# Decoder layers with a mixture of experts: the normalised rows are transposed last in a round of the token-expert stage, and the router products come one round later

## The chip, the cores and the metric

The kernel runs on one NeuronCore of one Trainium2 chip. The metric is the device time of one execution in microseconds (us). The engines that matter here are TensorE (PE: matmuls and transposes, with the weight loads apart as PEld), VectorE (DVE), ScalarE (ACT), GpSimd (POOL, which also issues the indirect transfers) and SyncE (SP, which issues the plain transfers). Each engine works through its own instructions in the order in which they are written, and waits at the head of its queue for the semaphores that the next instruction names.

## The reference

Three blocks on x of shape (4, 256, 256), each followed by a residual addition and a layer norm:

```
x = _layernorm(x + _L0_attn_ref(x, q_proj, k_proj, v_proj, o_proj))          # causal attention, 16 heads
x = _layernorm(x + _L0_xattn_ref(x, token_ids, ctx, ctx, ctx))               # expert by token id
x = _layernorm(x + _L0_ffn_ref(x, Wr, br, Wg, Wu, Wd))                       # top-1 expert by a router

# _L0_xattn_ref: expert_ids = min(clip(token_ids, 0, 12499) // 3125, 3); for the row's expert e
#   y = (silu(h @ Wg[e].T) * (h @ Wu[e].T)) @ Wd[e].T, here with all three = ctx (4, 256, 256)
# _L0_ffn_ref: probs = softmax(x @ Wr + br); top_w, top_idx = top_k(probs, 1)
#   out = top_w * ((silu(x @ Wg[top_idx]) * (x @ Wu[top_idx])) @ Wd[top_idx])
```

## The kernel before

The 1024 tokens are eight tiles of 128 rows. After attention (to about 118 us of the span) comes the **token-expert stage**, the second block of the reference. Six of the tiles have been scattered into rows that are sorted by expert and are read back as nine tiles of one expert each; the last two go through all four experts at once ("dense"). So the stage has NS = 11 tiles, of which numbers 3 and 6 are dense (DENSE_AT). Float32 products are made of three float16 products (hi*hi, hi*lo, lo*hi), so ScalarE writes a "hi" half and VectorE a "lo" half of every operand.

The stage is a software pipeline written out by hand. Each engine runs the same loop over rounds s = 0 to NS + 4; in round s the engines do different steps of different tiles, and every engine does its steps in the order of its own code:

- TensorE: T(s), two transposes of the tile's rows into bank 0 (L1513). T5(s-5), two transposes of the normalised rows into bank 5 (L1521), after a wait for `x2_rdy`. G(s-1), the gate product into bank 1 (L1263 through the helper `three`; six matmuls, for a dense tile twice six of 512 columns). T2(s-2), transposes of the gated rows into bank 2 (L1555; a dense tile: eight, L1499). D(s-3), the second product (L1263; a dense tile: 24 matmuls, L1576). R(s-5), the router product of four small matmuls (L1587), which waits for ScalarE's copy `x2T`.
- ScalarE: the hi half of T(s) (L670), the copy `x2T` of T5(s-5) (L677), SiLU of G(s-1) (L685; dense L693), the hi half of T2(s-2) (L701; dense L708). The latter waits until D of the sorted tile before has been done, since there is one buffer `hs_hi`.
- VectorE: the lo half of T(s) (L1105), SiLU times gate of tile s-1 (L1115; dense L1126), the lo half of T2(s-2) (L1134; dense L1090), the residual of tile s-3 (L1147), the normalisation of tile s-4 (L1152, which gives `x2_rdy`), the statistics of tile s-3 (L1156, L1158). Weight splits of the next stage (L552 on ScalarE, L779 on VectorE) lie in four places of the rounds.
- GpSimd: per tile the inverse deviation (L505, L506) that the normalisation waits for.

The router's work goes in two parts (PARTS): tiles 0 to 5 and tiles 6 to 10. For part 0, VectorE runs `logits` and `top_expert` (L825 to L843) at the start of round 11, ScalarE the exponentials (L661, with a table load) at the end of it, TensorE the counting product (L1256, L1257), and VectorE `top_weight` and `places` (L850 to L871) at the start of round 12; `places` gives `pos_rdy`. For part 1 all this follows after the last round. GpSimd's queue holds, in this order: the inverse deviations of tiles 0 to 8, the scatter of tile 0 (L512, waits for `places` of part 0), the inverse deviation of tile 9, the scatter of tile 1, the inverse deviation of tile 10, the scatters of tiles 2 to 5 and then those of tiles 6 to 10 (which wait for `places` of part 1). When all eleven have landed, the sorted tiles are read back and the third block runs (from about 195 us to the end), with TensorE busy nearly throughout.

Of the kernel before, what the change touches and what calls it, by code (L numbers as in the profile page):

```python
# [14 lines left out]
ALU, ACT, AX = mybir.AluOpType, mybir.ActivationFunctionType, mybir.AxisListType  # L15

P = 128
# [6 lines left out]
NK = D // P  # L24
# [24 lines left out]
NOWHERE = 8192.0  # L49
PARTS = ((0, 6), (6, NS))  # L50
# [14 lines left out]
def build(nc, x_tok, xT, ids, wqkvT, woT, ctxT, Wr, br, Wf, out):  # L65
    ctx = ExitStack()
    with ctx:
# [476 lines left out]
        def _(act):  # L544
# [118 lines left out]
            for s in range(NS + 5):  # L663
# [8 lines left out]
                i = s - 5  # L672
                if 0 <= i < NS:
                    act.wait_ge(x2T_rdy, i + 1)
                    if i >= 1:
                        act.wait_ge(lg_rdy, i)
                    a.activation(x2T, ps[:, 5, 0:D].rearrange("p (k t) -> p k t", k=NK),  # L677
                                 ACT.Copy).then_inc(x2T_sb, 1)
# [32 lines left out]
                if s - 3 in DENSE_AT:  # L711
                    split_hi(n)
                    n += 1
                for part, (_, last) in enumerate(PARTS[:-1]):
                    if s == last + 5:
                        exps_router(part)
# [51 lines left out]
        def _(dve):  # L768
# [325 lines left out]
            for s in range(NS + 5):  # L1094

                for part, (_, last) in enumerate(PARTS[:-1]):
                    if s == last + 5:
                        logits(part)
                        top_expert(part)
                    elif s == last + 6:  # L1100
                        top_weight(part)
                        places(part)
# [146 lines left out]
        def _(pe):  # L1249
# [253 lines left out]
            for s in range(NS + 5):  # L1503
# [11 lines left out]
                i = s - 5  # L1515
                if 0 <= i < NS:
                    pe.wait_ge(x2_rdy, i + 1)
                    if i >= 1:
                        pe.wait_ge(x2T_sb, i)
                    for k in range(NK):  # L1520
                        last = t.transpose(ps[:, 5, k * P:(k + 1) * P], XS[:, i, k * P:(k + 1) * P], identF[:, :])  # L1521
                    last.then_inc(x2T_rdy, 1)
# [56 lines left out]
                i = s - 5  # L1579
                if 0 <= i < NS:  # L1580
# [8 lines left out]
                    last.then_inc(lg_rdy, 1)  # L1589
                for part, (first, last) in enumerate(PARTS[:-1]):  # L1590
                    if s == last + 5:
                        pe.wait_ge(oh_rdy, part + 2)
                        count(PART_BANK[part], first, last)
# [121 lines left out]
```

## Time and profile before

| | us |
|---|---|
| three runs | 303.61, 306.0, 306.82 (median 306.0) |
| profiled execution, its own time | 303.86 |
| its span | 301.7 |
| around the span | 2.16 |
| PE / DVE / ACT / POOL busy | 239.1 / 193.3 / 135.8 / 66.8 |

"Busy" counts the time in which an engine has an instruction at work; matmuls overlap, so that a row's duration is longer than the step from its start to the next start, and that step is the price of an instruction in a full queue. In the timeline, the bracket at a row's end is the idle time of the engine just before it, and which instruction ended it. "PEclk" is the granted TensorE clock as a share of full speed: 1.00 is 2.4 GHz, and about 0.5 is 1.2 GHz.

### The profile page before, as it was taken

What the parts mean: (1) busy time and instruction counts of PE and PEld (TensorE: products, weight loads), DVE (VectorE), ACT (ScalarE), POOL (GpSimd) and SP (SyncE); (2) the same over time, 40 slices, a digit from 0 to 9 for tenths busy, and PEclk for the clock granted to TensorE, in tenths of its full rate; (3) what the DMA queues carried; (4) which work ended last, traced back from release to release, by engine and by line L of the source; (5) the groups of instructions that cost most, each with busy time, mean ns of one, the idle gap of its engine ahead of it and who ended that gap; (6) DMA issues with size and microseconds to landing.
All of it is one profiled execution on the core that took longest, in us unless ns stands there. A gap on an engine that the chain in (4) does not pass through costs nothing.

```text
span 301.7 us, 7078 instructions
## 1 busy us (share of the span) xinstructions
PE 239.1 (79%) x2714; PEld 192.2 (64%) x2730; DVE 193.3 (64%) x425; ACT 135.8 (45%) x229; POOL 66.8 (22%) x128
## 2 busy tenths in 40 slices
PE   4795598898988795778958575499696999999970
PEld 4363465665665563457747452199695999999960
DVE  4866858776797665576776835589645555555550
ACT  4460455765775964343534416177420333333300
POOL 8400000100032243122112286200022222222222
PEclk9797989999999999697999955999999999999996
DMA  6999216142043452411224902241000000000000
GB/s 207 332 281 299 74 45 253 59 139 70 3 141 107 118 165 98 130 27 45 77 66 134 412 24 88 79 121 41 2 20 0 21 13 21 21 20 20 2 8 14
DMA packets 17423, 28.62 MB, mean 95 GB/s; under 512 B 2733, under 2 KB 12974, under 8 KB 17392
## 3 DMA queue, kind: packets, MB, share of 16 engines
q1 hardware_dynamic: 16048, 25.28, 27.8%
q0 software_dynamic: 1344, 2.90, 2.7%
q8 instruction: 22, 0.36, 0.5%
q14 instruction: 9, 0.07, 0.1%
HBM read 19.43 MB, written 9.50 MB: 96 GB/s over the span
## 4 chain that ended last, share of the span: by engine, by line
PE 56%; DVE 21%; issue 8%; ACT 5%; DMA 4%; POOL 3%; SPq 1%; POOLq 0%; ACTq 0%; DVEq 0%
PE ps L1263 8%; PE ps L1632 7%; PE ps L1633 7%; PE ps L1634 7%; PE ps L1649 3%; PE ps L1651 3%; PE ps L1650 3%; PE ps L1334 3%; DVE arena L945 3%; PE ps L1373 2%; DVE wf_lo L779 2%; PE ps L1576 2%; PE ps L1521 2%; PE ps L1330 2%; DVE arena L1147 1%
## 5 line engine op out<-in xcount | busy, mean ns | idle before, releaser
L1632 PE MATMUL ps<-arena,wf_hi 128*128 128x128 f16 x352 | 60.2, 219 | 0.3 <-DVE arena L1175 0.3
L1633 PE MATMUL ps<-arena,wf_hi 128*128 128x128 f16 x352 | 60.3, 218 | 0.0
L1634 PE MATMUL ps<-arena,wf_lo 128*128 128x128 f16 x352 | 60.2, 217 | 0.0
L1633 PEld LDWEIGHTS ps<-arena,wf_hi 128*128 x352 | 34.3, 98 | 0.2
L1632 PEld LDWEIGHTS ps<-arena,wf_hi 128*128 x352 | 33.8, 96 | 0.9 <-issue 0.8
L1634 PEld LDWEIGHTS ps<-arena,wf_lo 128*128 x352 | 33.9, 96 | 0.0
L1649 PE MATMUL ps<-wf_hi,arena 128*128 x88 | 24.0, 273 | 5.9 <-DVE arena L1200 3.4
L779 DVE SCALAR_TENSOR_TENSOR wf_lo<-ring,wf_hi 128x1024 f16<-128x1024 f32 x17 | 20.6, 1220 | 12.5 <-ACT wf_hi L552 7.4
L735 ACT ACTIVATE arena<-ps 128x512 f32<-128x512 f32 x22 | 13.1, 595 | 29.7 <-PE ps L1634 29.7
L1650 PE MATMUL ps<-wf_lo,arena 128*128 x88 | 24.0, 273 | 0.0
L1651 PE MATMUL ps<-wf_hi,arena 128*128 x88 | 24.0, 273 | 0.0
L1263 PE MATMUL ps<-xT_hi,arena 128*128 (+1 forms) x88 | 23.1, 325 | 1.1 <-DVE arena L1115 1.1
L1184 DVE SCALAR_TENSOR_TENSOR arena<-ps,arena 128x512 f32<-128x512 f32 x22 | 15.2, 690 | 10.3 <-PE ps L1634 9.5
L742 ACT ACTIVATE arena<-arena 128x512 f16<-128x512 f32 x22 | 13.8, 629 | 16.6 <-DVE arena L1184 16.6
L1191 DVE TENSOR_TENSOR arena<-arena 128x512 f16<-128x512 f32 x22 | 15.2, 690 | 8.8 <-ACT arena L742 8.8
L945 DVE TENSOR_REDUCE arena<-ps 128x4 f16<-128x1024 f32 x16 | 19.6, 1223 | 1.6 <-PE ps L1334 1.6
L1263 PE MATMUL ps<-arena,xT_hi 128*128 128x512 f16 (+1 forms) x64 | 16.5, 348 | 2.7 <-DVE arena L900 1.9
L529 POOL TENSOR_SCALAR veps<-mv 128x1 f32<-128x1 f32 x11 | 2.5, 225 | 71.1 <-DVE mv L1206 71.1
L552 ACT ACTIVATE wf_hi<-ring 128x1024 f16<-128x1024 f32 x17 | 17.7, 1052 | 0.1
L599 ACT ACTIVATE arena<-ps 128x1024 f32<-128x1024 f32 x16 | 16.5, 1033 | 1.1 <-PE ps L1357 0.7
L940 DVE TENSOR_REDUCE arena<-ps 128x4 f16<-128x512 f32 x16 | 11.0, 689 | 8.0 <-PE ps L1334 7.8
L1334 PE MATMUL ps<-arena 128*128 128x128 f16 x144 | 13.8, 236 | 1.7 <-DVE wf_hi L926 1.0
(223 smaller groups left out, 568.1 us busy)
## 6 DMA issues: line engine op xcount, KB each, us to landing
ring<-Wf SPq DMA_DIRECT2D x17, 512.0 KB, 3.7
sorted<-fill SPq DMA_DIRECT2D x1, 4515.0 KB, 21.9
arena<-Wf SPq DMA_DIRECT2D x7, 512.0 KB, 7.2
arena<-sorted SPq DMA_DIRECT2D x20, 129.0 KB, 2.5
sorted<-fill SPq DMA_DIRECT2D x1, 1161.0 KB, 6.6
ring<-xT SPq DMA_DIRECT2D x4, 256.0 KB, 4.8
X<-x_tok SPq DMA_DIRECT2D x1, 1024.0 KB, 7.7
ring<-ctxT SPq DMA_DIRECT2D x2, 512.0 KB, 3.8
```

The source lines that it names most:

```text
L552: a.activation(chunk_dst(ORDER[n], True), src, ACT.Copy, scale=W_SCALE).then_inc(c_hi, 1)
L599: a.activation(Pf[n % 2][:, 1:3], ps[:, 4:6, :], ACT.Exp, scale=DK ** -0.5).then_inc(exped, 1)
L779: v.scalar_tensor_tensor(out=chunk_dst(ORDER[n], False), in0=staged(n)[0], scalar=W_SCALE, in1=chunk_dst(ORDER[n], True), op0=ALU.mult, op ...
L945: v.tensor_reduce(dst[:, 1], ps[:, 1:3, :].rearrange("p c (a k) -> p a c k", a=G), AX.XY, ALU.max, negate=True).then_inc(maxed, 1)
L1263: last = t.matmul(dst, xs(k), ws(k), start=(k == 0 and m == 0), stop=(k == nk - 1 and m == 2))
L1334: last = t.matmul(ps[:, bank, i * P:(i + 1) * P], q[:, h, qt * P:(qt + 1) * P], k[:, h // 2, kt * P:(kt + 1) * P], start=not diag, stop=(n ...
L1632: t.matmul(dst, hi, a_hi[p][:, k], start=k == 0, stop=False)
L1633: t.matmul(dst, hi, a_lo[p][:, k], start=False, stop=False)
L1634: last = t.matmul(dst, lo, a_hi[p][:, k], start=False, stop=k == NK - 1)
L1649: t.matmul(ps[:, 7, 0:D], hs[:, c], hi, start=c == 0, stop=False)
L1650: t.matmul(ps[:, 7, 0:D], hs[:, c], lo, start=False, stop=False)
L1651: last = t.matmul(ps[:, 7, 0:D], ls[:, c], hi, start=False, stop=c == NF - 1)
```

## The change

The constant LOGIT_LAG = 6 takes the place of the 5 in the length of the rounds and in the places of the router's work. Three things move. On TensorE the transposes T5(s-5) go from behind T(s) to the end of round s, and the router product in round s is that of tile s-6. On ScalarE the copy `x2T` of tile s-5 goes from the second place of the round to the last. On VectorE, ScalarE and TensorE the router work of part 0 (`logits`, `top_expert`, exponentials, count, `top_weight`, `places`) comes one round later, and there is one round more. GpSimd's and SyncE's instructions and their order stay as they are.

```
@@ -47,6 +47,7 @@
 NEG = -3.0e38
 PAD_TOKEN = 4096.0
 NOWHERE = 8192.0
+LOGIT_LAG = 6
 PARTS = ((0, 6), (6, NS))
 PART_BANK = (6, 7)
 AHEAD3 = 3
@@ -660,7 +661,7 @@
                 act.wait_ge(lg_sb, part + 1)
                 a.activation(ex[:, first:last, :], lg[:, first:last, :], ACT.Exp).then_inc(ex_rdy, 1)
 
-            for s in range(NS + 5):
+            for s in range(NS + LOGIT_LAG):
                 if s < NS:
                     act.wait_ge(a2T, s + 1)
                     if s >= 2:
@@ -669,13 +670,6 @@
                             act.wait_ge(bz, 2 * dense_before(s - 1))
                     a.activation(a_hi[s % 2], ps[:, 0, 0:D].rearrange("p (k t) -> p k t", k=NK),
                                  ACT.Copy).then_inc(a2hi, 1)
-                i = s - 5
-                if 0 <= i < NS:
-                    act.wait_ge(x2T_rdy, i + 1)
-                    if i >= 1:
-                        act.wait_ge(lg_rdy, i)
-                    a.activation(x2T, ps[:, 5, 0:D].rearrange("p (k t) -> p k t", k=NK),
-                                 ACT.Copy).then_inc(x2T_sb, 1)
                 i = s - 1
                 k, j = (sorted_of(i), dense_of(i)) if 0 <= i < NS else (None, None)
                 if k is not None:
@@ -711,8 +705,15 @@
                 if s - 3 in DENSE_AT:
                     split_hi(n)
                     n += 1
+                i = s - 5
+                if 0 <= i < NS:
+                    act.wait_ge(x2T_rdy, i + 1)
+                    if i >= 1:
+                        act.wait_ge(lg_rdy, i)
+                    a.activation(x2T, ps[:, 5, 0:D].rearrange("p (k t) -> p k t", k=NK),
+                                 ACT.Copy).then_inc(x2T_sb, 1)
                 for part, (_, last) in enumerate(PARTS[:-1]):
-                    if s == last + 5:
+                    if s == last + LOGIT_LAG:
                         exps_router(part)
             exps_router(len(PARTS) - 1)
             a.activation(sg[:, 0:1], identF[:, 0:1], ACT.Silu)
@@ -1091,13 +1092,13 @@
                                 h_hi[:, 4 * half:4 * half + 4], ALU.subtract).then_inc(bhlo, 1)
 
             inv = 1 / W_SCALE
-            for s in range(NS + 5):
+            for s in range(NS + LOGIT_LAG):
 
                 for part, (_, last) in enumerate(PARTS[:-1]):
-                    if s == last + 5:
+                    if s == last + LOGIT_LAG:
                         logits(part)
                         top_expert(part)
-                    elif s == last + 6:
+                    elif s == last + LOGIT_LAG + 1:
                         top_weight(part)
                         places(part)
                 if s < NS:
@@ -1500,7 +1501,7 @@
                                        identF[:, :])
                 last.then_inc(bhT, 1)
 
-            for s in range(NS + 5):
+            for s in range(NS + LOGIT_LAG):
                 if s < NS:
                     k = sorted_of(s)
                     if k is not None:
@@ -1512,14 +1513,6 @@
                     for k in range(NK):
                         last = t.transpose(ps[:, 0, k * P:(k + 1) * P], XS[:, s, k * P:(k + 1) * P], identF[:, :])
                     last.then_inc(a2T, 1)
-                i = s - 5
-                if 0 <= i < NS:
-                    pe.wait_ge(x2_rdy, i + 1)
-                    if i >= 1:
-                        pe.wait_ge(x2T_sb, i)
-                    for k in range(NK):
-                        last = t.transpose(ps[:, 5, k * P:(k + 1) * P], XS[:, i, k * P:(k + 1) * P], identF[:, :])
-                    last.then_inc(x2T_rdy, 1)
                 i = s - 1
                 k, j = (sorted_of(i), dense_of(i)) if 0 <= i < NS else (None, None)
                 if k is not None or j is not None:
@@ -1576,7 +1569,7 @@
                             last = t.matmul(ps[:, (3, 4)[i % 2], 0:D], xs[:, c], ws[:, c * D:(c + 1) * D],
                                             start=(c == 0 and m == 0), stop=(c == NF - 1 and m == 2))
                     last.then_inc(y2, 1)
-                i = s - 5
+                i = s - LOGIT_LAG
                 if 0 <= i < NS:
                     if i == 0:
                         pe.wait_ge(in_r, 32)
@@ -1587,8 +1580,16 @@
                         last = t.matmul(ps[:, bank, col * E:(col + 1) * E], x2T[:, k], wr_sb[:, k, :],
                                         start=(k == 0), stop=(k == NK - 1))
                     last.then_inc(lg_rdy, 1)
+                i = s - 5
+                if 0 <= i < NS:
+                    pe.wait_ge(x2_rdy, i + 1)
+                    if i >= 1:
+                        pe.wait_ge(x2T_sb, i)
+                    for k in range(NK):
+                        last = t.transpose(ps[:, 5, k * P:(k + 1) * P], XS[:, i, k * P:(k + 1) * P], identF[:, :])
+                    last.then_inc(x2T_rdy, 1)
                 for part, (first, last) in enumerate(PARTS[:-1]):
-                    if s == last + 5:
+                    if s == last + LOGIT_LAG:
                         pe.wait_ge(oh_rdy, part + 2)
                         count(PART_BANK[part], first, last)
             pe.wait_ge(oh_rdy, len(PARTS) + 1)
```

The places in the queues, as rows of the compiled kernels. First TensorE where round 9 ends and round 10 begins, before the change: the last matmul of a dense second product (L1576), the router product R(4), the transposes T(10) (L1513), then T5(5) (L1521), and the gate product G(9) (L1263; ISA and REGISTER_ALU set its address).

```order
L1576 MATMUL ps<-xT_hi,arena 128x256
L1587 MATMUL ps<-wr_sb,arena 128x4 x2
L1513 MATMUL ps<-identF,arena 128x128 x2
L1521 MATMUL ps<-identF,arena 128x128 x2
L1263 ISA
L1263 MATMUL ps<-xT_hi,arena 128x256
```

The same place after the change, where the lines are L1569 for the second product, L1580 for the router product (now R(3)), L1589 for T5 (now T5(4)), L1514 for T(10) and L1264 for G(9):

```order
L1569 MATMUL ps<-xT_hi,arena 128x256
L1580 MATMUL ps<-wr_sb,arena 128x4 x2
L1589 MATMUL ps<-identF,arena 128x128 x2
L1514 MATMUL ps<-identF,arena 128x128 x2
L1264 ISA
L1264 MATMUL ps<-xT_hi,arena 128x256
```

T5 now stands behind the products of its round, and nothing stands between T(10) and G(9). 

Second, ScalarE's queue in rounds 7 to 9 before the change: a_hi (L670), the copy x2T (L677), SiLU (L685), then the hi half of T2 (L708 for the dense tile, L701 else).

```order
L670 ACTIVATE arena<-ps 128x256
L677 ACTIVATE arena<-ps 128x256
L685 ACTIVATE arena<-ps 128x256
L708 ACTIVATE arena<-ps 128x512 x2
L670 ACTIVATE arena<-ps 128x256
L677 ACTIVATE arena<-ps 128x256
L685 ACTIVATE arena<-ps 128x256
L701 ACTIVATE arena<-ps 128x256
```

After the change (a_hi is L671, SiLU L679, the dense hi half L702, the other L695, the copy x2T L713):

```order
L671 ACTIVATE arena<-ps 128x256
L679 ACTIVATE arena<-ps 128x256
L702 ACTIVATE arena<-ps 128x512 x2
L713 ACTIVATE arena<-ps 128x256
L671 ACTIVATE arena<-ps 128x256
L679 ACTIVATE arena<-ps 128x256
L695 ACTIVATE arena<-ps 128x256
```

The copy has moved behind both steps that it stood ahead of.

Third, the end of the stage on TensorE before the change, from T5(8) on: the second product D(10), then R(8), T5(9), R(9), T5(10), R(10) and the count of part 1.

```order
L1521 MATMUL ps<-identF,arena 128x128 x2
L1263 MATMUL ps<-xT_hi,arena 128x256
L1263 MATMUL ps<-xT_lo,arena 128x256
L1263 MATMUL ps<-xT_hi,arena 128x256 x2
L1263 MATMUL ps<-xT_lo,arena 128x256
L1263 MATMUL ps<-xT_hi,arena 128x256
L1587 MATMUL ps<-wr_sb,arena 128x4 x2
L1521 MATMUL ps<-identF,arena 128x128 x2
L1587 MATMUL ps<-wr_sb,arena 128x4 x2
L1521 MATMUL ps<-identF,arena 128x128 x2
L1587 MATMUL ps<-wr_sb,arena 128x4 x2
```

After the change, from the count of part 0 on (L1257, L1258): D(10), R(7), T5(8), R(8), T5(9), R(9), and T5(10) and R(10) behind them.

```order
L1257 MATMUL ps<-oh,before 128x24
L1258 MATMUL ps<-oh,ones 128x24
L1264 MATMUL ps<-xT_hi,arena 128x256
L1264 MATMUL ps<-xT_lo,arena 128x256
L1264 MATMUL ps<-xT_hi,arena 128x256 x2
L1264 MATMUL ps<-xT_lo,arena 128x256
L1264 MATMUL ps<-xT_hi,arena 128x256
L1580 MATMUL ps<-wr_sb,arena 128x4 x2
L1589 MATMUL ps<-identF,arena 128x128 x2
L1580 MATMUL ps<-wr_sb,arena 128x4 x2
L1589 MATMUL ps<-identF,arena 128x128 x2
L1580 MATMUL ps<-wr_sb,arena 128x4 x2
```

The count of part 0 now stands ahead of D(10), one round later than before, and the order of the last three tiles' transposes and router products among themselves is the same.

## Rows read from the trace of the kernel before

**Rows 1.** Waits between 118 and 185 us: waiter <- releaser: total us, times, longest.

```profile
PE ps L1521 <- DVE arena L1152: 11.5, 10, 2.1
```

**Rows 2.** Busy time and granted clock by stretch (stretch, length, busy by engine, PEclk, DMA).

```profile
136.20:139.70 3.50, 3.44 (x17) 3.04 (x18) 1.26 (x5) 1.35 (x3) 0.79 (x2) 0.51 0.12 48
139.70:173.60 33.90, 24.71 (x206) 20.50 (x203) 25.95 (x78) 15.62 (x34) 5.70 (x15) 1.00 0.43 154
173.60:184.20 10.60, 6.00 (x26) 4.56 (x26) 5.31 (x28) 4.04 (x8) 7.73 (x10) 0.51 0.15 51
```

**Rows 3.** Timeline, TensorE, rounds 5 and 6: start, us, line, idle before.

```profile
133.79 0.38 PE L1513 MATMUL ps<-identF,arena 128*128 128x128 f32 x2
136.26 0.69 PE L1521 MATMUL ps<-identF,arena 128*128 128x128 f32 x2 [2.09 <-DVE arena L1152]
...
140.72 0.42 PE L1513 MATMUL ps<-identF,arena 128*128 128x128 f32 x2
```

**Rows 4.** Timeline, VectorE, around the dense tile 3.

```profile
133.57 1.65 DVE L1126 SCALAR_TENSOR_TENSOR arena<-ps,pick,arena 128x256 f32<-128x256 f32 x4
135.14 0.41 DVE L1134 TENSOR_TENSOR arena<-ps,arena 128x256 f16<-128x256 f32 x1
```

**Rows 5.** Timeline, TensorE, rounds 7 to 10, at full clock.

```profile
146.97 0.38 PE L1263 MATMUL ps<-xT_hi,arena 128*128 128x512 f16 x1
...
149.56 0.38 PE L1555 MATMUL ps<-identF,arena 128*128 128x128 f32 x2
...
153.44 1.04 PE L1499 MATMUL ps<-identF,arena 128*128 128x128 f32 x8
154.32 0.27 PE L1263 MATMUL ps<-xT_hi,arena 128*128 x1
...
157.86 0.44 PE L1521 MATMUL ps<-identF,arena 128*128 128x128 f32 x2 [2.10 <-DVE arena L1152]
158.13 0.27 PE L1263 MATMUL ps<-xT_hi,arena 128*128 x1
...
158.79 0.38 PE L1555 MATMUL ps<-identF,arena 128*128 128x128 f32 x2
159.00 0.27 PE L1576 MATMUL ps<-xT_hi,arena 128*128 128x256 f16 x1
...
161.62 0.51 PE L1587 MATMUL ps<-wr_sb,arena 128*128 128x4 f32 x4
161.99 0.42 PE L1513 MATMUL ps<-identF,arena 128*128 128x128 f32 x2
```

**Rows 6.** Timeline, all engines, rounds 11 and 12: from D(8) to the next T5.

```profile
167.47 0.27 PE L1263 MATMUL ps<-xT_hi,arena 128*128 x1
...
168.79 1.28 ACT L661 ACT_TABLE_LOAD   x1
168.81 0.42 DVE L1134 TENSOR_TENSOR arena<-ps,arena 128x256 f16<-128x256 f32 x1 [0.23 <-ACT arena L701]
...
169.94 0.44 PE L1521 MATMUL ps<-identF,arena 128*128 128x128 f32 x2 [1.25 <-DVE arena L1152]
170.09 0.22 ACT L661 ACTIVATE ex<-lg 128x24 f32<-128x24 f32 x1
...
170.35 0.16 DVE L850 TENSOR_SCALAR off<-valid 128x6 f32<-128x6 f32 x1
```

**Rows 7.** Timeline, all engines, the tail: places of part 0 to the scatter of tile 6.

```profile
172.42 0.17 DVE L871 TENSOR_TENSOR pos_i<-pos,off 128x6 int32<-128x6 f32 x1
...
173.44 1.10 POOL L512 DMA_INDIRECT sorted<-arena,pos_i  x1 [2.04 <-DVE pos_i L871]
...
174.90 0.57 POOL L506 TENSOR_TENSOR rstd<-veps,minus_half 128x1 f32<-128x1 f32 x1
...
177.85 0.41 DVE L1152 TENSOR_SCALAR arena<-arena,mv,rstd 128x256 f32<-128x256 f32 x1 [1.01 <-POOL rstd L506]
...
185.02 0.97 POOL L512 DMA_INDIRECT sorted<-arena,pos_i  x1 [1.97 <-DVE pos_i L871]
```

More of the change, by code:

```diff
@@ L49 @@
 NOWHERE = 8192.0
+LOGIT_LAG = 6
 PARTS = ((0, 6), (6, NS))
@@ L661, in exps_router @@
                 a.activation(ex[:, first:last, :], lg[:, first:last, :], ACT.Exp).then_inc(ex_rdy, 1)
-            for s in range(NS + 5):
+            for s in range(NS + LOGIT_LAG):
                 if s < NS:
@@ L671, in _ @@
                                  ACT.Copy).then_inc(a2hi, 1)
[L672 to L678, printed above, removed]
                 i = s - 1
@@ L713, in _ @@
                     n += 1
+                i = s - 5
+                if 0 <= i < NS:
+                    act.wait_ge(x2T_rdy, i + 1)
+                    if i >= 1:
+                        act.wait_ge(lg_rdy, i)
+                    a.activation(x2T, ps[:, 5, 0:D].rearrange("p (k t) -> p k t", k=NK),
+                                 ACT.Copy).then_inc(x2T_sb, 1)
                 for part, (_, last) in enumerate(PARTS[:-1]):
-                    if s == last + 5:
+                    if s == last + LOGIT_LAG:
                         exps_router(part)
@@ L1093, in _ @@
             inv = 1 / W_SCALE
-            for s in range(NS + 5):
+            for s in range(NS + LOGIT_LAG):
                 for part, (_, last) in enumerate(PARTS[:-1]):
-                    if s == last + 5:
+                    if s == last + LOGIT_LAG:
                         logits(part)
                         top_expert(part)
-                    elif s == last + 6:
+                    elif s == last + LOGIT_LAG + 1:
                         top_weight(part)
@@ L1501, in dense_T @@
                 last.then_inc(bhT, 1)
-            for s in range(NS + 5):
+            for s in range(NS + LOGIT_LAG):
                 if s < NS:
@@ L1514, in _ @@
                     last.then_inc(a2T, 1)
[L1515 to L1522, printed above, removed]
                 i = s - 1
@@ L1578, in _ @@
                     last.then_inc(y2, 1)
-                i = s - 5
+                i = s - LOGIT_LAG
                 if 0 <= i < NS:
@@ L1589, in _ @@
                     last.then_inc(lg_rdy, 1)
+                i = s - 5
+                if 0 <= i < NS:
+                    pe.wait_ge(x2_rdy, i + 1)
+                    if i >= 1:
+                        pe.wait_ge(x2T_sb, i)
+                    for k in range(NK):
+                        last = t.transpose(ps[:, 5, k * P:(k + 1) * P], XS[:, i, k * P:(k + 1) * P], identF[:, :])
+                    last.then_inc(x2T_rdy, 1)
                 for part, (first, last) in enumerate(PARTS[:-1]):
-                    if s == last + 5:
+                    if s == last + LOGIT_LAG:
                         pe.wait_ge(oh_rdy, part + 2)
```

## The prediction

> **What bounds the kernel now.** I read the waits of the token-expert stage first, then its timeline on TensorE, then the rows of the tail across all engines. TensorE stands still for T5, the transposes of the normalised rows, in ten of eleven rounds, 11.5 us in all, and every time VectorE's normalisation (L1152) ends the wait [rows 1]. The longest waits are 2.09 and 2.10 us [rows 3, 5]. The reader is to see in rows 6 what such a wait consists of: TensorE begins D(8) at 167.47, ScalarE and VectorE turn the gated rows into halves (VectorE from 168.81), then VectorE does residual and normalisation, and T5(7) begins at 169.94. T5 stands near the head of a round, so it waits for the last link of the round before, and the products behind it, which need none of that, wait too. From 172.42 on another chain sets the end: `places` of part 0, then GpSimd's queue (scatter, inverse deviation of tile 9, scatter, inverse deviation of tile 10), then the normalisation of tile 10 at 177.85, its router product, and the scatter of tile 6 at 185.02 [rows 7]. Everything behind that scatter keeps its instructions and its order, so I take it to shift as one piece.
>
> **Prices.** From starts of neighbours in a full queue at full clock [rows 5]: a gate product G and a second product D of a sorted tile (the same six matmuls) 0.66 us (158.13 to 158.79); a dense gate product 2.59 (146.97 to 149.56); a dense second product 2.62 (159.00 to 161.62); T2 0.21; dense T2 0.88 (153.44 to 154.32); a router product R 0.37 (161.62 to 161.99); T5 0.27 (157.86 to 158.13), and T, which has the same shape, as much. A semaphore from one engine to the next I count as 0.05 us (168.81 to 169.94 holds three links in line and leaves no more).
>
> **Round 5 after the change.** T(5) begins at 133.79 as before [rows 3] and costs 0.27. G(4) then needs only the first half of VectorE's dense gating, four instructions from 133.57 in 1.65 us, so half of it by 134.40 [rows 4]: it runs from 134.45 to 135.11. The dense T2 needs the lo half of tile 2, ready at 135.14 + 0.41 = 135.55 [rows 4]: from 135.60, 0.88 long. D(2) adds 0.66, T5(0) 0.27, so T(6) begins at 137.41 instead of 140.72 [rows 3]: 3.3 us earlier. The wait of 2.09 has shrunk to two of 0.39 and 0.49, R(0) has gone to the next round (0.37), and the stretch at half clock from 136.2 to 139.7 (0.51, [rows 2]) is assumed gone. That is worth 3.50 x 0.49 = 1.7 us of the 3.3. Two ends: it stays (0 of the 1.7), or it goes (all). I take the latter, because the stretch followed directly on the idle 2.09 us and TensorE now idles 0.9 us there in two pieces; the rest of the stage ran at 1.00 although TensorE waited in it [rows 2].
>
> By the Trainium skill ("TensorE: Matmul & The Clock Gate", Part 1: The HAM clock gate) the half rate is the default and activity of the engine releases it, so by the page too the early stretch would go; but it speaks against the thin end of the stage, where the engine has little to do from round 11 on and could fall to half rate sooner. The trace agrees with the first half in that the 0.51 follows a wait [rows 2, 3]; it does not bear out that every such wait lowers the clock, since the 2.10 us at 157.86 did not [rows 2, 5].
>
> **Rounds 6 to 11.** With no wait for T5, a round costs TensorE what it issues. Round 6: T, G, T2, dense D, R, T5 = 0.27 + 0.66 + 0.21 + 2.62 + 0.37 + 0.27 = 4.40. Round 7 (dense gate): 4.37. Round 8 (dense T2): 3.11. Round 9 (dense D): 4.40. Round 10: 2.44. Round 11, without T: 2.17. Sum 20.89, so round 12 begins at 158.30; before, it began with T5(7) at 169.94 [rows 6].
>
> Is that cover real? The next thing to be late is T2 or D, which wait for the lo half of the tile before. From D's start to that half takes 168.81 + 0.42 + 0.05 - 167.47 = 1.81 us [rows 6]. Between D and the next T2, TensorE now issues D, R, T5, T and G = 2.23 us in rounds 6 to 10, and 1.96 without T in round 11: cover of 0.42 and 0.15 us. In round 12 neither T nor G is left: 1.30 us, so T2(10) waits 0.5. T5 itself has the whole round as cover for residual and normalisation. If the cover were gone, each round would pay the difference. The copy `x2T` costs nothing in its new place: what is queued behind it on ScalarE is a_hi of the next round and the SiLU of the next G, and both need TensorE work that stands behind T5 anyway. R(s-6) finds the copy done a round ago.
>
> **Part 0 of the router, one round later.** Round 12: 158.30 + 0.5, T2(10) 0.21, D(9) 0.66, R(6) 0.37, T5(7) begins at 160.04 and ends at 160.48. ScalarE must copy it (0.4) before the exponentials, table load and all 1.30 + 0.22 [rows 6]: done at 162.4. VectorE: D(8) begins at 157.00, so its lo half at 157.00 + 1.34 = 158.34, and 1.54 us later (168.81 to 170.35, [rows 6]) its next round: 159.88. `logits` and `top_expert` are eight small instructions; the twelve from 170.35 to 172.42 [rows 6, 7] have a step of 0.19, so 1.5 us: 161.4. Residual, normalisation and statistics, 1.54 again: 162.95. The exponentials are ready, so `top_weight` and `places` run, L871 starting 2.07 later at 165.0. Before: 172.42. So 7.4 us earlier; without the added round it would have been some 3 us more (the logits and 1.54 of VectorE).
>
> **The tail.** GpSimd's scatter of tile 0 waits for `places`, and the inverse deviation of tile 9 is queued behind it, then the next scatter, then that of tile 10. Before, the normalisation of tile 10 began 177.85 - 172.42 = 5.43 us after L871, with GpSimd as releaser [rows 7]. Now tile 9's has to wait for the same chain: it begins 3.1 us after L871 (174.90 + 0.57 + 0.05 - 172.42), at 168.1. Tile 10's statistics follow it by 169, while GpSimd is still in the second scatter. So tile 10 is normalised at 165.0 + 5.43 = 170.4, and R(9), at half clock about 1 us, ends by 170.7, before T5(10) can start at 170.9. The new wait of some 4 us ahead of T5(9) is parallel to this chain and costs nothing. From there to the scatter of tile 6 it is 7.17 us as before [rows 7]: 177.6 against 185.02.
>
> **Sum.** -7.4 us against the profiled execution, 303.86, gives 296.5. That execution is a low one: it and the three runs (303.61, 306.0, 306.82) have a mean of 305.1, 1.2 above it. I do not know which level the next runs take and add the 1.2: 297.7. Against the median of 306.0 the same sum would give 298.6.
>
> **Rivals.**
> 1. The forecast, chance 0.69: 7.4 us less, own range 295.5 to 299.
> 2. Part of it is eaten, chance 0.19. Either half clock stays in round 5 or comes at the thin end: +1.7 for the stretch of rows 2, and up to +2.2 where round 11 runs at half rate. Or the cover of 0.42 us is too small: 0.3 us in each of six rounds is +1.8. Times 299.4 to 302. For: the clock did fall twice in this stage [rows 2]; VectorE is busy 25.95 of 33.9 us [rows 2], and my rounds leave it less air. Against: VectorE's share of the 31.7 us from T(6) to L871 is 24.3 us, and I give that work 27.6.
> 3. The waits only move, chance 0.07: T2 and D wait for their halves about 1 us in each round, and the added round eats the rest; 302.9 to 306.
> 4. The change is slower, chance 0.05. The mechanism is GpSimd's queue: if the rounds kept their length, `places` of part 0 would come one round later, 3.6 us (T5, G, T2 = 1.14 and 169.94 - 167.47 = 2.47, [rows 6]), and with it scatter, tile 9, tile 10 and part 1. That gives 307.5 by the profiled execution, 308.7 at the level of my forecast. It decides as soon as rounds 5 to 12 give back less than 3.6 of the 11.5 us. Against it: G needs nothing of the normalisation, by code and by rows 4.
>
> That the change does nothing is part of 3; the order of TensorE's rows excludes that T5 still holds up its own round.
>
> **Range and chances.** 295.0 takes the lower level of the runs with 1.5 us more than the sum; 301.5 takes the half clock and most of the lost cover. What a measurement here can tell from no change is about 1%, 3 us. Faster by over 1% (below 302.9): 0.88. Within: 0.07. Slower: 0.05.
>
> **What would show it.** TensorE's wait for L1152 is gone in rounds 5 to 12 and there is one long wait, about 4 us, ahead of T5(9). T(6) begins near 137.4, L871 of part 0 near 165.0, and the scatter of tile 6 near 177.6; the granted clock is 1.00 from 136.2 on. Wrong would be: waits of T2, D or G for VectorE of more than 0.3 us in each round, 0.5 in PEclk after 134, L871 later than 168, or more than 5.5 us from it to the normalisation of tile 10.

## The result, and the profile after

The changed kernel takes 294.31 us (median of 294.12 to 296.42, four runs) against 306.41 us of the kernel before (303.61 to 309.97) in the same measurement. The ratio is 0.9717, 95% interval 0.9676 to 0.9759: 2.8% faster. (The ratios here compare undisturbed runs only, so they are not the quotients of the medians.) On a second chip it took 299.05 us (298.75 to 299.61) against 304.2, ratio 0.9845 (0.977 to 0.9919). The sign is the same, the size is not, and the experiments below have to say why.

| | before, profiled | after, profiled |
|---|---|---|
| its own time / span | 303.86 / 301.7 | 294.23 / 292.2 |
| T(0) begins | 120.85 | 120.20 |
| T(0) to T(5) | 12.94 | 11.67 |
| T(5) to the scatter of tile 6 | 51.23 | 43.56 |
| from there to the last scatter | 5.11 | 5.11 |
| last scatter to the end | 111.57 | 111.66 |

T(5), with which round 5 begins, is the last thing on TensorE ahead of the first moved instruction. So 7.67 of the 9.5 us between the spans lie where the change is, and 1.9 us ahead of it, in code that both kernels share.

The waits of TensorE for the normalisation answer to [rows 1]; the first row shown is GpSimd's wait for the places. Waits from 118 to 178 us of the changed kernel (waiter <- releaser: total us, times, longest):

```profile
POOL sorted L513 <- DVE pos_i L872: 7.0, 2, 5.1
...
PE ps L1589 <- DVE arena L1153: 4.2, 2, 4.0
```

11.5 us in ten waits have become 4.2 us in two, and the long one of 4.0 stands in the tail, beside GpSimd's chain, where it costs nothing of its own. Here is TensorE's timeline in round 5 and at the start of round 6, which answers to [rows 3]:

```profile
131.87 0.38 PE L1514 MATMUL ps<-identF,arena 128*128 128x128 f32 x2
...
132.68 0.28 PE L1264 MATMUL ps<-xT_hi,arena 128*128 x1 [0.43 <-DVE arena L1127]
...
133.60 1.09 PE L1500 MATMUL ps<-identF,arena 128*128 128x128 f32 x8
...
135.18 0.38 PE L1589 MATMUL ps<-identF,arena 128*128 128x128 f32 x2
135.40 0.38 PE L1514 MATMUL ps<-identF,arena 128*128 128x128 f32 x2
```

T(5) to T(6) is 3.53 us; it was 6.93. The one wait that these rows name is for VectorE's dense gating (L1127), ahead of G(4). A second, of some 0.26 us ahead of the dense T2, can be read from the starts only (133.60 against 132.68 + 0.66, the price of G). Here are all waits of TensorE between 133 and 166 us that the same timeline shows, one after the other:

```profile
156.73 0.44 PE L1548 MATMUL ps<-identF,arena 128*128 128x128 f32 x2 [0.38 <-DVE arena L1135]
159.44 0.19 PE L1257 MATMUL ps<-oh,before 128*128 128x24 f16 x1 [1.00 <-DVE oh L844]
159.86 0.27 PE L1264 MATMUL ps<-xT_hi,arena 128*128 x1 [0.21 <-DVE arena L1135]
161.77 0.61 PE L1580 MATMUL ps<-wr_sb,arena 128*128 128x4 f32 x4 [0.47 <-ACT arena L713]
```

From 134 to 156 there is none: rounds 6 to 11 run nearly on what TensorE issues. The tail, all engines, answers to [rows 7]:

```profile
162.88 0.17 DVE L872 TENSOR_TENSOR pos_i<-pos,off 128x6 int32<-128x6 f32 x1
...
163.89 1.09 POOL L513 DMA_INDIRECT sorted<-arena,pos_i  x1 [5.05 <-DVE pos_i L872]
...
165.34 0.57 POOL L507 TENSOR_TENSOR rstd<-veps,minus_half 128x1 f32<-128x1 f32 x1
165.95 0.41 DVE L1153 TENSOR_SCALAR arena<-arena,mv,rstd 128x256 f32<-128x256 f32 x1 [2.57 <-POOL rstd L507]
...
166.42 0.69 PE L1589 MATMUL ps<-identF,arena 128*128 128x128 f32 x2 [4.04 <-DVE arena L1153]
...
168.30 0.41 DVE L1153 TENSOR_SCALAR arena<-arena,mv,rstd 128x256 f32<-128x256 f32 x1 [1.38 <-POOL rstd L507]
...
175.43 0.97 POOL L513 DMA_INDIRECT sorted<-arena,pos_i  x1 [1.92 <-DVE pos_i L872]
```

The scatter of tile 0 has been waited for (5.05 us), the inverse deviation of tile 9 runs behind it, and VectorE (2.57) and TensorE (4.04) wait in turn. The clock by stretch answers to [rows 2]; the third number from the end is PEclk:

```profile
134.00:140.00 6.00, 6.00 (x58) 5.51 (x57) 5.93 (x16) 3.39 (x8) 1.58 (x4) 1.00 0.10 41
140.00:158.00 18.00, 17.62 (x150) 14.77 (x148) 16.32 (x46) 10.31 (x25) 3.98 (x11) 1.00 0.49 162
...
164.00:176.00 12.00, 4.95 (x18) 3.06 (x19) 5.68 (x32) 5.06 (x8) 8.46 (x11) 0.50 0.13 43
```

The stretch at half clock (1.2 GHz) in round 5 is gone, and TensorE is busy 17.62 of 18 us in the middle of the stage.

### The profile page after: what moved, and what is told of

It is laid out like the page before. It is cut to its first block, busy times and chain, and to the rows that moved or that the text cites. A ratio compares the mean times of both kernels' runs of the same rounds, so it can differ in the third digit from the quotient of the medians.

```text
span 292.2 us, 7078 instructions
## 1 busy us (share of the span) xinstructions
PE 233.1 (80%) x2714; PEld 188.0 (64%) x2730; DVE 192.3 (66%) x425; ACT 135.0 (46%) x229; POOL 66.8 (23%) x128
## 4 chain that ended last, share of the span: by engine, by line
PE 56%; DVE 18%; issue 9%; DMA 5%; ACT 5%; POOL 4%; SPq 1%; POOLq 0%; DVEq 0%; ACTq 0%
PE ps L1264 8%; PE ps L1633 7%; PE ps L1634 7%; PE ps L1635 7%; PE ps L1650 3%; PE ps L1652 3%; PE ps L1651 3%; PE ps L1335 3%; PE ps L1374 2%; DVE arena L946 2%; PE ps L1569 2%; POOL sorted L513 2%; PE ps L1331 2%; DVE arena L941 2%; ACT wf_hi L553 1%
## 5 line engine op out<-in xcount | busy, mean ns | idle before, releaser
L1264 PE MATMUL ps<-xT_hi,arena 128*128 (+1 forms) x88 | 20.5, 299 | 1.1 <-DVE arena L1127 0.4
L1264 PE MATMUL ps<-arena,xT_hi 128*128 128x512 f16 (+1 forms) x64 | 15.8, 337 | 2.5 <-DVE arena L901 1.8
L534 POOL DMA_INDIRECT out<-arena,out_i x11 | 12.0, 1091 | 13.8 <-DVE arena L1213 13.8
```

Source lines behind the costliest of these rows:

```text
L1264: last = t.matmul(dst, xs(k), ws(k), start=(k == 0 and m == 0), stop=(k == nk - 1 and m == 2))
```

## The experiments

**All profiled executions in one table.** The four columns, with the 5.1 us from the scatter of tile 6 to the last scatter (5.09 to 5.13 in all rows), make up the whole span. "Stage" is from T(5) to the scatter of tile 6; "rest" is from the last scatter to the end, and its code is the same in all rows except where dummies were put in.

```
                             T(0) at  T(0)-T(5)  stage   rest    half clock in the rest at
before                        120.9     12.94    51.23   111.57  -
before, dummies in stage 3    121.3     13.03    51.34   111.56  -
before, dummies in rounds     121.0     11.70    49.51   111.55  -
before, GpSimd reordered      119.8     10.99    52.83   113.83  192, 216
after                         120.2     11.67    43.56   111.66  -
after, again                  122.0     11.71    43.62   115.36  186 to 192, 210
after, dummies in stage 3     121.2     12.95    43.66   113.16  222
T5 early                      120.3     10.99    56.19   111.60  -
copy early                    121.3     10.99    58.11   113.12  220 to 224
no lag                        120.7     11.00    46.64   113.56  186, 210
T5 twice                      118.9     12.93    45.09   113.63  184 to 188, 208
lo half twice                 121.4     12.94    46.47   113.63  188, 212
GpSimd: scatters last         120.3     10.99    41.43   113.04  180 to 186
GpSimd, dummies               120.4     12.94    40.96   111.62  -
```

The stage repeats to 0.1 us where the code is the same (two rows of the kernel before, three of the changed one). The two columns beside it do not: 11.0 to 13.0, and 111.6 to 115.4. So the stage is what the theories are judged by, and the times of whole runs say less. That the two rows of the kernel before agree is in part luck: the first row has half clock from 136.2 to 139.7 us, behind the wait in round 5, the second from 156 to 160 us, behind the one in round 9, one stretch each. "Dummies" are matmuls that only keep TensorE busy; nothing reads their results.

### The changed kernel again

No edit.

> The changed kernel itself, on the same chip as the next three, so that they can be held against it. All theories: the ratio to the kernel before is 0.972 again. In the trace the stretch from T(5) to the scatter of tile 6 is 43.6 us (51.2 before). What happens ahead of T(5) is the same code in both kernels: if the first profile's 1.9 us there was only the phase in which the clock rose, this stretch differs from run to run; if it belongs to the change, T(5) begins at 131.9 again and not near 133.8.

Measured: 299.05 us against 304.2 (ratio 0.9845, where 0.972 was expected). The stage took 43.62 us, as in the first profile (43.56). T(5) began at 133.7, as in the kernel before (133.8) and not at 131.9: the 1.9 us ahead of the stage were not the change's. The kernel was slower than on the first chip in the rest: 115.36 us instead of 111.66. The profile of this run there (busy by engine; the third number from the end is PEclk):

```profile
186.00:192.00 6.00, 5.22 (x34) 3.69 (x33) 3.84 (x4) 2.27 (x3) 0.00 (x0) 0.51 0.43 114
192.00:208.00 16.00, 16.00 (x271) 15.83 (x269) 12.49 (x18) 12.01 (x20) 0.00 (x0) 0.97 0.19 52
208.00:210.40 2.40, 0.04 (x1) 0.00 (x0) 2.40 (x4) 1.29 (x2) 0.00 (x0) 0.92 0.00 0
210.40:213.00 2.60, 2.52 (x12) 1.80 (x13) 0.51 (x1) 0.00 (x0) 0.00 (x0) 0.50 0.00 0
```

After each of two waits TensorE worked for some us at half clock. The same waits stand in the first profile, 3.2 us for the scatters and 2.4 us ahead of the first down product, and there the clock stayed at full speed behind them.

### T5 back at the head of the round, the rest as changed

```
                     last.then_inc(a2T, 1)
+                i = s - 5
+                if 0 <= i < NS:
+                    pe.wait_ge(x2_rdy, i + 1)
...
-                i = s - 5
-                if 0 <= i < NS:
-                    pe.wait_ge(x2_rdy, i + 1)
```

(with the two transposes of T5 behind the wait in both places)

> The changed kernel with T5 back behind T(s) on TensorE; the router products stay one round later and ScalarE's copy stays last. Theory (T5's wait at the head of the round was the brake): the gain is gone, the wait for the normalisation is back in every round, and the added round costs a little: 0 to +1 us against the kernel before, near 306. Rival (the gain comes from ScalarE's order, or from the router products that no longer wait for their copy): most of the 8 to 9 us stays, near 298.

Measured: 309.69 us (305.95 to 324.67), ratio 1.0198 (1.0085 to 1.0312): slower than before. Waits from 128 to 180 us:

```profile
PE ps L1522 <- DVE arena L1153: 15.0, 9, 4.8
```

The wait is back, 15.0 us of it. Without the move on TensorE nothing of the gain is left; the rival falls. I had expected at most 1 us of loss. In the trace T(5) to L872 is 42.8 us against 38.6 of the kernel before: the router's part 0 comes one round later, the price that the forecast's fourth rival put at 3.6 us, and here nothing pays for it. But the clock fell to 0.5 around 136 and 156, two stretches against the one of the kernel before. The kernel before with GpSimd's queue reordered (below) has two such stretches at the same places and takes 39.4 us over this distance. Against that row the added round costs 3.4 us, and the rest of the 4.2 goes with the second stretch.

### ScalarE's copy back in second place

```
                                  ACT.Copy).then_inc(a2hi, 1)
+                i = s - 5
+                if 0 <= i < NS:
+                    act.wait_ge(x2T_rdy, i + 1)
...
-                i = s - 5
-                if 0 <= i < NS:
-                    act.wait_ge(x2T_rdy, i + 1)
```

(with the copy x2T behind the wait in both places)

> The changed kernel with ScalarE's copy x2T back in second place of the round, ahead of SiLU and of the hi half; TensorE as changed. Theory (each engine waits at the head of its queue): the copy of round s waits for T5 at the end of TensorE's round, with SiLU(s-1) and the hi half behind it, so that all engines run in turn: from T(5) to the scatter of tile 6 some 59 us instead of 43.6, the kernel 7 to 9 us slower than before, near 314. Rival (ScalarE is only 45% busy and its order hardly matters): within 2 us of the changed kernel, near 298.

Measured: 311.41 us, ratio 1.0281 (1.0193 to 1.037); the stage took 58.11 us, 14.5 more than with the copy last. Waits from 128 to 180 us:

```profile
ACT arena L678 <- PE ps L1589: 29.2, 9, 6.3
DVE arena L1116 <- ACT arena L686: 13.0, 7, 3.9
...
PE ps L1264 <- DVE arena L1116: 6.1, 5, 1.4
```

The forecast of this run was a stage of some 59 us. ScalarE (133.6 us busy of 308.6) stands 29.2 us in front of the copy, VectorE waits for the SiLU behind it, and TensorE's next gate product waits for VectorE. The move on TensorE needs the move on ScalarE: the low busy share of ScalarE did not make its order harmless. The clock stood at half between 149 and 156 us too; how much of the 14.5 us that is was not measured.

### Router products in the same round, directly behind T5

```
-LOGIT_LAG = 6
+LOGIT_LAG = 5
```

(and on TensorE the block of T5 stands ahead of that of R, both at the end of the round)

> The changed kernel without the later router products: T5 behind D, then at once R of the same tile, LOGIT_LAG = 5. Theory: R waits for ScalarE's copy in every round, about 0.5 us with TensorE idle, and one round is saved: of the gain of 7.7 us some 3 us is left, near 303. Rival (the lag only costs a round, since part 0 comes later): faster than the changed kernel by up to 3 us, near 294.

Measured: 299.55 us, ratio 0.9872 (0.9797 to 0.9948). The stage took 46.64 us: 3.1 more than changed, 4.6 less than before. Waits of the trace from 128 to 180 us:

```profile
PE ps L1588 <- ACT arena L713: 6.7, 11, 1.3
```

Eleven waits for the copy, 6.7 us, against one round saved; neither kernel has half clock between T(5) and 164 us. The rival, that the lag is pure cost, falls: the lag is worth 3.1 us net. The expectation had put 4.7 us on it (3 left of 7.7), so its sign was right and its size half too large.

### GpSimd: the scatters behind the inverse deviations

```
-            for i in range(NS - 2):
+            for i in range(NS):
                 inv_std2(i)
-            scatter3(0, 0)
-            inv_std2(NS - 2)
-            scatter3(0, 1)
-            inv_std2(NS - 1)
```

(and the loop behind it then issues all scatters.)

> The changed kernel with GpSimd's queue reordered: all inverse deviations first, then the scatters of tiles 0 to 10. Theory (in the tail, the scatters of tiles 0 and 1 stand ahead of the inverse deviations of tiles 9 and 10, and that chain now sets the end): normalisation of tile 10 some 2.8 us earlier, the scatters then follow one another without a gap, and the last one begins 2.5 us earlier: 2 to 3 us faster than the changed kernel, ratio to the kernel before near 0.964. Rival (the chain is hidden behind the last products, or the scatters are the bound anyway): no difference to the changed kernel, 0.972.

Measured: 292.43 us, ratio 0.9641 (0.9584 to 0.9698), and a stage of 41.43 us, 2.1 less than in the changed kernel (2.5 expected). GpSimd's timeline, where the first of these scatters is that of tile 0:

```profile
164.09 0.57 POOL L507 TENSOR_TENSOR rstd<-veps,minus_half 128x1 f32<-128x1 f32 x1
164.92 1.15 POOL L513 DMA_INDIRECT sorted<-arena,pos_i  x1 [0.27 <-issue]
166.38 0.97 POOL L513 DMA_INDIRECT sorted<-arena,pos_i  x1 [0.30 <-issue]
...
177.86 0.97 POOL L513 DMA_INDIRECT sorted<-arena,pos_i  x1 [0.30 <-issue]
```

From L868 (162.32, the places of part 0) to the normalisation of tile 10 (164.69) it now takes 2.4 us instead of 5.4. The gap ahead of the scatter of tile 6 has gone, and the eleven scatters run one behind the other at 1.28 us: now GpSimd's issue is what ends last. The rival of a hidden chain falls.

### The same on the kernel before

> The same reordering of GpSimd's queue in the kernel before. Theory: there the normalisations of tiles 9 and 10 came late for another reason too (the products), so that little is to be had: -0.5 to +0.5 us, ratio 1.00. Rival (the scatters ahead of the inverse deviations cost the kernel before as much as the changed one): 2 to 3 us faster, ratio 0.992.

Measured: 305.58 us (301.74 to 307.1) against 303.75 (301.5 to 308.35); no ratio is on record, and the spreads overlap. The stage took 52.83 us instead of 51.23, 1.6 more, where -0.5 to +0.5 was expected. Here the order is no gain. The first of the eleven scatters now starts at 175.8, behind the inverse deviation of tile 10, and that of tile 6 comes at 183.6, 1.63 us after its places (L867 at 181.95) where it was 0.96 in the kernel before: 0.7 us is the queue's. The other 0.9 had come by those places, and what differs up to there is a half-clock stretch around 156, which the first profile does not have. The same edit is worth 2.1 us in one kernel and nothing in the other. The traces show why: in the old one GpSimd could begin the inverse deviation of tile 9 at 171.98 only, on the release of its statistics, 1.8 us after the places of part 0 (L867 at 170.19); in the changed kernel those statistics are written at 160.74, 2.1 us ahead of the places, and the scatter of tile 0 is all that the inverse deviation still stands behind.

### T5 issued twice

```
-                    for k in range(NK):
+                    for k in (0, 1, 0, 1):
```

> The changed kernel with the two transposes of T5 issued twice in each round (the same data into the same place, output unchanged): 0.27 us more of TensorE's issue time a round. Theory (TensorE's issue time now sets the round, by the prices of the forecast): eight rounds ahead of L872 pay it, +1.9 to +2.5 us against the changed kernel. Rival (VectorE sets the round now): below 0.7 us.

Measured: 297.83 us (294.28 to 300.4); the ratio to the kernel before, 0.972, is that of the changed kernel, so that the price shows in the trace alone: the stage took 45.09 us, 1.5 more than changed. The step from T5 to T in the trace is 0.47 us instead of 0.25, so that each doubling costs 0.22, not 0.27, and T(5) to T(10) grows from 19.73 to 20.60 us in five rounds, by 0.2 in four of them. Of the 1.5 us, 1.0 have come by L872; the other 0.5 are T5(9) and T5(10) at half clock. Both my figure (1.9 to 2.5) and the rival's (below 0.7) miss. The direction speaks for TensorE as the bound of rounds 5 to 8, where the extra time comes through whole (round 9 takes 4.53 us before and 4.55 with it); in rounds 11 and 12 most of it disappears in the wait for the lo half (0.16 us left of 0.38 in the trace).

### The lo half written twice

```
+                    link(v.tensor_tensor(hs_lo, ps[:, 2, 0:D].rearrange("p (k t) -> p k t", k=NK),
+                                         hs_hi, ALU.subtract))
                     v.tensor_tensor(hs_lo, ps[:, 2, 0:D].rearrange("p (k t) -> p k t", k=NK),
                                     hs_hi, ALU.subtract).then_inc(h2lo, 1)
```

> The changed kernel with VectorE's lo half of each sorted tile written twice, the first time waited for: 0.43 to 0.46 us more of VectorE a round, just ahead of the lo half that T2 and D wait for (output unchanged). Theory (this link has a cover of 0.42 us in rounds with T and G behind D, 0.15 in round 11 and none after): +2.5 to +3.3 us, most of it in rounds 10 to 13 and in the round with the dense T2. Rival (VectorE has slack, 16.3 us busy of 18): below 1 us. Rival (VectorE is the bound): 9 x 0.45 = 4 us.

Measured: 301.36 us (ratio 0.9894, 0.9837 to 0.995); the stage took 46.47 us, 2.9 more, as the theory said. The timeline of TensorE has these waits for the written halves (L1137), and none for them between the second and the third:

```profile
137.04 1.09 PE L1502 MATMUL ps<-identF,arena 128*128 128x128 f32 x8 [0.55 <-DVE arena L1137]
148.85 1.09 PE L1502 MATMUL ps<-identF,arena 128*128 128x128 f32 x8 [0.31 <-DVE arena L1137]
...
161.61 0.44 PE L1550 MATMUL ps<-identF,arena 128*128 128x128 f32 x2 [0.83 <-DVE arena L1137]
...
165.20 0.37 PE L1266 MATMUL ps<-xT_hi,arena 128*128 x1 [0.65 <-DVE arena L1137]
```

From T to T, rounds 6, 7 and 9 take 4.35, 4.30 and 4.53 us with and without the doubling: the cover takes it whole there. The 2.9 us come from round 5 (1.0, VectorE being late with the dense gating too), the round with the dense T2, and rounds 11 to 13, where no T or no G lies between D and the next T2. I had not named round 5. Both rivals fall (below 1 us, and 4 us).

### The kernel before with dummies in two waits of its rounds

```
                 i = s - 5
+                if i in (0, 4):
+                    keep_warm(8, wf_hi[:, 0:512], bank=5)
```

> The kernel before with 8 dummy matmuls ahead of T5(0) and of T5(4), in the two waits of about 2.1 us; order unchanged. It prices the clock alone. Theory: the stretches at half clock in rounds 5 and 9 are gone; from T(5) to the scatter of tile 6 it takes 49.3 to 49.9 us instead of 51.2 (52.8 in the run with both stretches), so the clock is 1.3 to 1.9 us of the 7.7. Rival (most of the gain is the clock that stays high when TensorE no longer waits): 45 us or less.

Measured: 303.17 us, ratio 0.9983 (0.9932 to 1.0033); the stage took 49.51 us, 1.7 less than before. No half clock in rounds 5 to 11:

```profile
127.00:170.00 43.00, 35.69 (x275) 27.43 (x274) 32.86 (x96) 21.07 (x46) 8.03 (x18) 1.00 0.36 125
```

So the clock is 1.7 us of the 7.67, as the forecast had it, and 6.0 are left for the order. The rival, that the clock is most of it, falls. In the time of whole runs the 1.7 us disappear in the spread.

### Dummies in the third stage, after and before

```
-            keep_warm(2 * WARM_GAP, wf_hi[:, 0:512])
+            keep_warm(26, wf_hi[:, 0:512])
...
                 if i == 0:
+                    keep_warm(8, wf_hi[:, 0:512], bank=5)
                     pe.wait_ge(c_lo, NCH)
```

> The changed kernel with idle TensorE time of the third stage filled: 26 instead of 16 dummy matmuls behind pos_rdy of part 1, and 8 ahead of the first down product (whose wait for VectorE's split was 2.4 us). Nothing else moves. Theory (from the scatter of tile 10 to the end the same code took 111.7, 113.0 and 115.4 us, because half clock followed these two waits in some executions and not in others): the stretches at half clock around 188 and 210 us are gone, the remainder is 111.7 us, and the runs lie near 294 with a small spread. Rival (the difference between 294 and 299 of the changed kernel is another chip or another cause): 297 to 300 as on the second chip, with or without dummies.

> The kernel before with the same dummy matmuls in the third stage. Theory: it too runs at its lower level, 302 to 304, and the two filled kernels differ by what the change does in its own stage, 7.6 us or 2.5%, with less spread than the unfilled pair. Rival (part of the gain of the first measurement lay in the third stage): the two filled kernels differ by 5 us or less.

Measured: 296.99 us for the changed kernel (295.24 to 298.31), where near 294 was expected and 297 to 300 was the rival's; 303.86 for the one before (300.67 to 305.53, ratio 1.0007). In both profiles the clock stays up at the two filled places, but in the changed kernel half clock came at another one, behind the wait of the third down product for VectorE. TensorE's timeline there:

```profile
222.42 0.39 PE L1651 MATMUL ps<-wf_hi,arena 128*128 x1 [2.74 <-DVE arena L1201]
```

That wait stands in every profile, and in no other one is there half clock behind it. So the expectation that the spread would go fails: the dummies move the place, and whether fewer such stretches come cannot be told from one profile each. The two filled kernels differ by 6.9 us in their medians, and by 7.7 in the stage (51.34 against 43.66), so that the second expectation's rival (5 us or less) falls.

### Both additions together

The dummies of the third stage, 5 more ahead of T5(9), and only the scatter of tile 0 ahead of the inverse deviation of tile 10:

```
-            for i in range(NS - 2):
+            for i in range(NS - 1):
                 inv_std2(i)
             scatter3(0, 0)
-            inv_std2(NS - 2)
-            scatter3(0, 1)
             inv_std2(NS - 1)
```

> The changed kernel with three additions: GpSimd's queue with only the scatter of tile 0 ahead of the inverse deviation of tile 10 and all other scatters behind it, the dummies of the third stage, and 5 dummies in the wait ahead of T5(9). Theory: L872 to the normalisation of tile 10 in 3.2 us instead of 5.4; the last scatter begins 3.5 us earlier than in the changed kernel, 45 us after T(5) instead of 48.7; the remainder is 111.7 us, so 290 us. Rival (the scatters are now the bound, 11 x 1.28 us from L872 on, whatever is ahead of them): no better than the run with all scatters last, 46.5 us.

Measured: 294.2 us (292.13 to 296.72), ratio 0.9708 (0.9573 to 0.9843), where 290 was expected. The places of part 0 (L870) to the normalisation of tile 10 took 3.1 us, as expected (3.2), and the rest 111.62. But the stage took 40.96 us, only 0.5 less than with all scatters last: T(5) to the last scatter is 46.1 us instead of 46.5, not the 45 that I had put on it. The scatters now follow one another without a gap and are the bound, as the rival said. This is the shortest stage of all kernels, but its time is not better than the 292.43 us of the simpler edit, measured on another chip with an overlapping spread; which of the two is faster is open.

## Why the prediction was right, step by step

**What bounded the kernel: right.** T5's wait for the last link of the round before was the brake. Putting T5 back brings the wait (15.0 us) and takes the whole gain away.

**Round 5: right.** Forecast 3.62 us from T(5) to T(6), measured 3.53. The half clock was taken to go, worth 1.7; it went, and the dummies in the kernel before measure 1.7. Both waits of the forecast came, split otherwise (0.54 and 0.26 us for 0.39 and 0.49, read from starts and prices): G(4) began 1.12 us after the dense gating (forecast 0.88), the dense T2 2.04 us after it (forecast 2.03), each counted from the start of L1127 at 131.56.

**Rounds 6 to 11: right to 0.1 us.** The forecast gave 20.89 us from T(6) to the start of round 12. T5(6) began at 155.94 and takes a step of 0.25, so TensorE was free at 156.19, 20.79 us after T(6) at 135.40. The cover of 0.42 us held too, as the doubled lo half shows. In round 12, T2(10) began at 156.73, 0.54 us after TensorE was free, forecast 0.5 (the bracket of 0.38 counts from the end of T5's own duration).

**One round later: right.** L872 came 31.01 us after T(5), forecast 31.2 (165.0 - 133.79).

**Tail: right.** L872 to the normalisation of tile 10 took 5.42 us, forecast 5.43; the new wait of 4.04 us ahead of T5(9) cost nothing, forecast "some 4". From there to the scatter of tile 6, 7.13 against 7.17.

**The sum: 7.4 forecast, 7.67 measured** for what the change touches. Against the 306.0 us shown, the ratio 0.9717 gives 297.3 us, 0.4 from the forecast of 297.7. That closeness is in part luck: the ratio stands for 8.7 us, of which the changed stage holds 7.67, and the rest lies in code that both kernels share.

**What was mis-sized is the level, not the change.** The first measurement's own median, 294.31, is 3.4 us below 297.7 and 0.7 below the low end. The step that failed is the last: I added 1.2 us because the profiled execution seemed a low one, and took everything ahead of T(5) and behind the scatter as fixed. Neither is. In the table of the profiled executions, T(0) to T(5) varies by 2.0 us and the rest by 3.8 us in shared code, and wherever it is longer, the trace has half clock there. The mean granted clock of each timed run tells it too: the kernel before takes 301.0 to 302.5 us at a mean clock of 0.945 to 0.952 and 303.2 to 305.4 at 0.934 to 0.936; the changed kernel takes 294.1 to 294.4 at 0.945 to 0.950, 296.4 at 0.934 and 298.8 to 299.6 at 0.921 to 0.933. Near 0.947 the two differ by 6.6 to 8.4 us, which holds the stage's 7.7. On the second chip the medians are only 5.2 us apart, and the changed kernel's four runs there had the lower clocks (0.921 to 0.933) beside 0.929 to 0.947 for most runs of the kernel before. Why half clock fell to one kernel more than to the other in that measurement is not settled.

**Rivals.** Eaten in part (0.19): no; the cover was real and the clock stayed up to the end of round 11 and beyond; in the tail it was 0.50 (164 to 176 us), as before the change (0.51 from 173.6 us, [rows 2]). Waits that only move (0.07): no. Slower (0.05): not here, but its mechanism is real: with T5 early, the round's delay cost 3.4 us at equal clock (forecast 3.6) and 4.2 with one more stretch at half clock, and the kernel was slower than before.

## What to carry to other kernels

In a pipeline written out by hand, look for the instruction at the head of an engine's round that waits for the last link of another engine's round, and move it behind the work that needs nothing of it; then count, from starts of neighbours, what lies between each product and its next reader, since that is the cover which is left. The reader of the moved result has to move with it on every engine: with the transposes or the copy left in its old place this kernel was slower than before, and the copy's old place cost 14.5 us in the stage, on an engine that is busy less than half of the time. The later router products are worth 3.1 us more. Judge such a change by the distance between two instructions around it in the trace, not by two medians, when the clock elsewhere moves the whole time by several us from one execution to the next.

## What the runs showed of the hardware

Equal waits of TensorE were followed by half clock in one execution and not in the next: the 2.4 us ahead of the first down product in the changed kernel (0.50 behind it in the second profile, 1.00 in the first), the 2.7 us ahead of the third (0.50 behind it in one profile of fourteen). In the rest a stretch lasted 3 to 7 us, and with one or two of them it took 1.4 to 3.8 us more. By the Trainium skill ("TensorE: Matmul & The Clock Gate", Part 1: The HAM clock gate) activity of the engine releases the half rate, and the moment of the release varies from run to run of one kernel. The traces agree: ahead of T(5), in code that both kernels share, the half clock lasted 6.8 us in the profile of the kernel before (122.6 to 129.4), 3.6 us in the first one of the changed kernel (122.7 to 126.3), and did not come in the rows that take 11.0 us from T(0) to T(5). They show besides that the fall back to half clock behind a wait varies in the same way, and that in one profile it came at a third wait after two had been filled with dummy matmuls. I had taken the kernel's clock outside the changed stage as a constant, and it is worth as much as half of the change.
